# Attention values computed in strips of TensorE's columns, with the softmax scaling ahead of them

## What is computed

```python
# layer 0: layer norm with a conditioned scale and shift, 16 heads of 32, 4 key/value heads
scores = einsum('bhtd,bhsd->bhts', q, k_exp) / sqrt(32)
scores = where(mask, -inf, scores)      # window of 64, every 64th key, no later block of 128
y = einsum('bhts,bhsd->bhtd', softmax(scores), v_exp)
x = x + y @ Wo0.T
# layer 1: RMS norm with a conditioned scale, 8 heads of 64, 1 key/value head, no mask
ctx = einsum('bkgst,bktd->bkgsd', softmax(q k^T / 8), v)
x = x + ctx @ Wo1.T
x = x + silu(h @ Wg.T) * (h @ Wu.T) @ Wd.T      # 2048 inner features
```

## Time and profile before

| | us |
|---|---|
| median of three runs | 1804.08 |
| the profiled execution: its span | 1804.9 |
| TensorE busy | 1717.2 (95%) |
| VectorE busy | 1152.3 (64%) |
| ScalarE busy | 945.9 (52%) |
| GpSimd busy | 398.8 (22%) |
| a steady round (pairs 2 to 7) | about 210 |

### The profile page before, as it was taken

One profiled execution on the slowest core, in us unless ns is written; L12 is line 12 of the kernel. 1 busy time (PEld: TensorE's weight loads), 2 busy tenths in 40 slices (PEclk: granted clock), 3 DMA queues, 4 the chain that ended last, 5 costly groups with the idle time before them and its releaser, 6 DMA issues.

```text
span 1804.9 us, 37773 instructions
## 1 busy us (share of the span) xinstructions
PE 1717.2 (95%) x12440; PEld 931.9 (52%) x12440; DVE 1152.3 (64%) x2858; ACT 945.9 (52%) x2769; POOL 398.8 (22%) x556
## 2 busy tenths in 40 slices
PE   6686899999999999999999999999999999999999
PEld 2344445555455545555455554555455554555444
DVE  6759566675667657685576756676576855767320
ACT  3836456364664538564483646645385644835320
POOL 3438587011111112111110111111121111101120
PEclk9676999999999999999999999999999999999999
DMA  7866489462784449662593637944485725936220
GB/s 245 152 181 115 126 197 253 98 117 82 163 175 94 80 119 184 133 118 78 127 194 91 119 88 161 171 95 82 115 192 125 123 73 138 196 85 112 100 70 24
DMA packets 527231, 234.30 MB, mean 130 GB/s; under 512 B 476336, under 2 KB 493744, under 8 KB 527024
## 3 DMA queue, kind: packets, MB, share of 16 engines
q1 hardware_dynamic: 511472, 175.09, 48.9%
q10 hardware_dynamic: 15552, 56.63, 10.1%
HBM read 90.09 MB, written 16.78 MB: 59 GB/s over the span
## 4 chain that ended last, share of the span: by engine, by line
PE 77%; DVE 10%; DMA 6%; issue 4%; ACT 2%; SPq 1%; DVEq 0%; POOL 0%; ACTq 0%
PE up L1427 8%; PE up L1429 8%; PE up L1428 8%; PE gate L1427 7%; PE gate L1429 7%; PE gate L1428 7%; PE y L1427 4%; PE y L1428 4%; PE y L1429 4%; PE bank L1427 4%; PE bank L1429 4%; PE bank L1428 4%; DMA prob_t<-prob 3%; PE bank L1454 2%; DVE prob L1113 2%
## 5 line engine op out<-in xcount | busy, mean ns | idle before, releaser
L864 ACT ACTIVATE bank<-bank,low 128x128 f32<-128x128 f32 (+2 forms) x768 | 302.7, 395 | 68.2 <-DVE low L1106 35.0
L702 POOL TENSOR_TENSOR inner_t<-inner,inner_t 128x512 f16<-128x512 f32 x128 | 149.0, 1164 | 662.7 <-ACT inner_t L1045 662.6
L1113 DVE TENSOR_TENSOR prob<-bank,prob 128x512 f16<-128x512 f32 (+1 forms) x320 | 202.8, 634 | 54.3 <-ACT prob L873 53.4
L873 ACT ACTIVATE prob<-bank 128x512 f16<-128x512 f32 (+1 forms) x320 | 178.7, 558 | 73.3 <-DMA prob_t<-prob 44.5
L1427 PE MATMUL up<-mlp,ring 128*128 128x512 f16 x512 | 194.9, 381 | 12.8 <-DVE inner L1392 12.8
L1382 DVE SCALAR_TENSOR_TENSOR silu<-silu,gate 128x512 f32<-128x512 f32 x128 | 87.9, 687 | 183.8 <-ACT silu L1039 183.0
L1427 PE MATMUL gate<-mlp,ring 128*128 128x512 f16 x512 | 194.0, 379 | 1.4 <-DVE mlp L1078 0.9
L1429 PE MATMUL up<-mlp,ring 128*128 128x512 f16 x512 | 194.9, 381 | 0.0
L1428 PE MATMUL up<-mlp,ring 128*128 128x512 f16 x512 | 194.9, 381 | 0.0
L1429 PE MATMUL gate<-mlp,ring 128*128 128x512 f16 x512 | 194.0, 379 | 0.0
L1428 PE MATMUL gate<-mlp,ring 128*128 128x512 f16 x512 | 193.9, 379 | 0.0
(11 more groups left out here) (182 smaller groups left out, 4041.8 us busy)
## 6 DMA issues: line engine op xcount, KB each, us to landing
ring<-wgu_dram ACTq DMA_DIRECT2D x108, 512.0 KB, 3.8
x_in<-x_dram SPq DMA_DIRECT2D x18, 512.0 KB, 3.8
x_res<-x_mid SPq DMA_DIRECT2D x16, 512.0 KB, 3.0
wgu_dram<-ring SPq DMA_DIRECT2D x16, 512.0 KB, 3.6
out_dram<-x_res SPq DMA_DIRECT2D x32, 256.0 KB, 2.3
prob_t<-prob SPq DMA_TRANSPOSE x256, 3.5
inner_t<-wd_t_dram SPq DMA_DIRECT2D x4, 1024.0 KB, 8.7
ring<-wg_t_dram SPq DMA_DIRECT2D x16, 256.0 KB, 4.1
```

What stands on the lines that cost most here:

```text
L702: pool.tensor_tensor(inner_t[:, 1, f, :], inner[:], inner_t[:, 0, f, :], ALU.subtract).then_inc(inner_low, 1)
L864: ins = act.activation(bank_[:, at:at + wid], bank_[:, at:at + wid], ACT.Exp, bias=low[:, j % BANKS, k:k + 1], scale=-1.0, accum_out=total)
L873: act.activation(terms(prob[:, g % SLOTS, 0, :], layer, j), terms(work_bank[USE[f"unit{layer}", j] % BANKS][:], layer, j), ACT.Copy).then_ ...
L1113: dve.tensor_tensor(terms(prob[:, slot, 1, :], layer, j), terms(work_bank[USE[name] % BANKS][:], layer, j), terms(prob[:, slot, 0, :], lay ...
```

## The change

1. **Values in strips.** The values are now the stationary operand, 32 columns wide in layer 0 and 64 in layer 1, and the turned exponentials move past them, 512 or 256 columns at a time. The four key/value heads of layer 0 write to four different sets of 32 partitions of one bank, the two halves of layer 1's heads to two sets of 64. Four units make a batch (`batch_values`); units are ordered so that a batch belongs to one sequence and one set of 128 tokens.
2. **Scaling earlier.** The result now has the features in the partitions, as the projection wants it, so the division can no longer follow. `inverses` takes the reciprocals of a unit's sums on VectorE, and `prob_highs` and `prob_lows` scale by them, one instruction for each head.
3. **Gone:** `normalise` and the transposes `heads` on TensorE. ScalarE and VectorE split the result straight from its bank.
4. **Moved:** the output projection of the first 128 tokens, and its `add`, stand at the last two units of a layer, and not behind them.
5. **Beside it:** the turned exponentials have eight places and not five; the weight `wo0` has its rows in another order and is split on GpSimd; squares go to other buffers.

The core of the diff:

```diff
 UNIT = [
-    [(s, 0, [(4 * g + j, j * P, P) for j in range(4)]) for g in range(4) for s in BOTH]
-    + [(s, 1, [(2 * k + j, 2 * j * P, K_TWO) for j in range(2)]) for k in range(8) for s in BOTH],
+    [(s, 0, [(4 * g + j, j * P, P) for j in range(4)]) for s in BOTH for g in range(4)]
+    + [(s, 1, [(4 * g + 2 * pair + j, 2 * j * P, K_TWO) for j in range(2)])
+       for pair in range(2) for s in BOTH for g in range(4)],
     [(s, t, [(2 * k + j, j * TOK, TOK) for j in range(2)])
-     for t in range(TILES) for k in range(4) for s in BOTH]]
+     for t in range(TILES) for s in BOTH for k in range(4)]]
...
+BATCH = 4
+BATCHES = [units // BATCH for units in UNITS]
...
+TAKE_AT = [{BATCH * last_batch(layer, s, 0) + BATCH - 1 + LAG + 1: s for s in BOTH}
+           for layer in range(2)]
+OUT_AT = [{22: 0, 23: 1}, {14: 0, 15: 1}]
...
             def prob_highs(n, layer, j):
                 g = unit_index(layer, j)
-                need(act, terms_made, count(n, sum(UNITS), g + 1))
+                need(act, inv_ready, count(n, sum(UNITS), g + 1))
                 turned_before(act, n, g)
-                act.activation(terms(prob[:, g % SLOTS, 0, :], layer, j),
-                               terms(work_bank[USE[f"unit{layer}", j] % BANKS][:], layer, j),
-                               ACT.Copy).then_inc(hi_done, 1)
+                s, t, columns = UNIT[layer][j]
+                bank_ = work_bank[USE[f"unit{layer}", j] % BANKS]
+                for h, at, wid in columns:
+                    ins = act.activation(prob[:, g % SLOTS, 0, at:at + wid], bank_[:, at:at + wid],
+                                         ACT.Copy, scale=inv[:, s, t, h:h + 1])
+                ins.then_inc(hi_done, 1)
...
+                        if j in TAKE_AT[layer]:
+                            heads(n, layer, TAKE_AT[layer][j], 0)
...
             def prob_lows(n, layer, j):
                 name, slot = (f"unit{layer}", j), unit_index(layer, j) % SLOTS
                 need(dve, hi_done, count(n, HI_USES, HI_USE[name] + 1))
-                dve.tensor_tensor(terms(prob[:, slot, 1, :], layer, j),
-                                  terms(work_bank[USE[name] % BANKS][:], layer, j),
-                                  terms(prob[:, slot, 0, :], layer, j),
-                                  ALU.subtract).then_inc(prob_split, 1)
+                s, t, columns = UNIT[layer][j]
+                bank_ = work_bank[USE[name] % BANKS]
+                for h, at, wid in columns:
+                    ins = dve.scalar_tensor_tensor(
+                        prob[:, slot, 1, at:at + wid], bank_[:, at:at + wid],
+                        inv[:, s, t, h:h + 1], prob[:, slot, 0, at:at + wid], ALU.mult,
+                        ALU.subtract)
+                ins.then_inc(prob_split, 1)
+
+            def inverses(n, layer, j):
+                s, t, columns = UNIT[layer][j]
+                heads = slice(columns[0][0], columns[-1][0] + 1)
+                need(dve, terms_made, count(n, sum(UNITS), unit_index(layer, j) + 1))
+                dve.reciprocal(inv[:, s, t, heads],
+                               (sums0 if layer == 0 else sums1)[:, s, t, heads]).then_inc(
+                                   inv_ready, 1)
...
+                inverses(n, layer, 0)
...
+                    if j + 1 < total:
+                        inverses(n, layer, j + 1)
+                    if j in TAKE_AT[layer]:
+                        heads_low(n, layer, TAKE_AT[layer][j], 0)
+                    if j in OUT_AT[layer]:
+                        add(n, layer, OUT_AT[layer][j], 0)
...
             def finish(n, m, layer):
                 between(m, f"out{layer}a.0", f"out{layer}a.1")
-                for s in BOTH:
-                    add(n, layer, s, 0)
-                for s in BOTH:
-                    normalise(n, layer, s, 1)
                 between(m, f"heads{layer}.0", f"heads{layer}.1")
                 for s in BOTH:
...
+            HALVES = ((0, 0), (0, 1), (1, 0))
+
+            def batch_values(n, layer, b):
+                first = BATCH * b
+                s, t, _ = UNIT[layer][first]
+                for j in range(first, first + BATCH):
+                    g = unit_index(layer, j)
+                    need(pe, prob_in[g % TURNED], turned_count(n, g))
...
+                turned = turned_batch(batch_index(layer, b))
+                if layer == 0:
+                    heads = UNIT[0][first][2]
+                    out_cols = slice(heads[0][0] % 4 * P, (heads[-1][0] % 4 + 1) * P)
+                    blocks = ([(P, 0, slice(0, 4))] if t == 0 else
+                              [(P, 1, slice(0, 4, 2)), (K_NEAR, 2, slice(1, 4, 2))])
+                    for m, (rows, tile, places) in enumerate(blocks):
+                        for k, (of_v, of_p) in enumerate(HALVES):
+                            for g in range(KV0):
+                                ins = pe.matmul(
+                                    ybank[s][g * HD0:(g + 1) * HD0, out_cols],
+                                    v0[s][of_v][0:rows, tile, g * HD0:(g + 1) * HD0],
+                                    turned[0:rows, g, of_p, places, :], start=m == 0 and k == 0,
+                                    stop=m == len(blocks) - 1 and k == 2)
+                else:
+                    for m in range(TILES):
+                        for k, (of_v, of_p) in enumerate(HALVES):
+                            for j in range(2):
+                                ins = pe.matmul(
+                                    ybank[s][j * HD1:(j + 1) * HD1, :], v1[s][of_v][:, m, :],
+                                    turned[:, :, of_p, 2 * j + m, :], start=m == 0 and k == 0,
+                                    stop=m == TILES - 1 and k == 2)
                 ins.then_inc(pv_done, 1)
...
-                    if j in FILL_AT[layer]:
-                        heads(n, layer, FILL_AT[layer][j], 0)
-                    if j >= LAG:
-                        unit_values(n, layer, j - LAG)
+                    if j in OUT_AT[layer]:
+                        project(n, layer, OUT_AT[layer][j], 0, w)
+                    if (j - LAG) % BATCH == BATCH - 1 and j >= LAG:
+                        batch_values(n, layer, (j - LAG) // BATCH)
...
             def finish(n, m, layer, w):
-                last = range(UNITS[layer] - LAG, UNITS[layer])
-                for s in BOTH:
-                    unit_values(n, layer, last[s])
-                    between(m, f"out{layer}a.{s}")
-                    project(n, layer, s, 0, w)
-                for j in last[PAIR:]:
-                    unit_values(n, layer, j)
+                between(m, f"out{layer}a.0")
+                between(m, f"out{layer}a.1")
+                batch_values(n, layer, BATCHES[layer] - 1)
                 for s in BOTH:
                     between(m, f"heads{layer}.{s}")
-                    heads(n, layer, s, 1)
```

148 lines of the change are left out of this document (49 added, 99 removed).

## The result

The changed kernel takes 1952.05 us (median of four runs, 1949.3 to 1958.9), the kernel before 1803.69 beside it: 1.083 times as long, 95% interval 1.081 to 1.085. The forecast was 1971, slower. The profiled execution has a span of 1951.2 us against 1804.9.

The account below looks back on a forecast made before the run. Bound: the ScalarE-VectorE chain in the units, not TensorE. Six steady rounds (131 us) plus 18 for each of two others gave +167 on the 1804.9 span: 1972, as median 1971 us; range 1890 to 2035.

Parts of the forecast that it names:

- The chain: In the units, reciprocal, high halves, low halves and minima take turns between VectorE and ScalarE; 1971 us, chance 0.68 with concurrent strips.
- The steady round: Sum for one round with feed-forward: 14.3 + 9.7 + 1.3 - 3.4 = +21.9 us, six of them 131.
- Prices of the chain: Turns of 3.5 (four heads), 2.3 (two heads) and 2.5 us (layer 1); layer 0 +14.3, layer 1 +9.7 us.
- A turn with a gate: Layer 0: VectorE waits for a tanh begun behind the high halves, then needs 0.6 us itself; 1.08 each, eight gates 8.6.
- Edges: Layers' first units +0.8 and +0.5 us; TensorE's work behind the last units 2.1 less in layer 0, 1.3 in layer 1.
- The first two rounds: The round with the second pair and the one without feed-forward (no gates, cheaper minima): 18 us more each.
- Strips side by side: TensorE's value matmuls run four at a time in layer 0, two in layer 1; TensorE's sum 8.7 us less a round.
- a rival at 1734 us: TensorE stays the bound, ScalarE and VectorE keep their overlap across units, strips run concurrently: 1734 us, faster; chance 0.04.
- Moved projections: First tokens' projections run at the last two units in TensorE's waiting time; two projections, 5.2 us, remain behind the last unit.
- The profile's signs: TensorE's share some 85%, idle before scores; high halves wait for the reciprocal, low halves for high halves in nearly every unit.
- that sign: The prediction would be wrong if PEclk, TensorE's granted clock, stood under 1.00 in the units.
- the rival's 20 us a round: TensorE's clock falls in layer 1's units, 60 us against 39.6: 8 x 20 more, 2134 us; chance 0.06.

Follow-up runs that it names:

- the open kernel: Changed kernel, but ScalarE's high halves wait only for their unit's exponentials, not for VectorE's reciprocal, and are left unscaled by the row sum: 1817.0 us.

## Why the prediction was right

**The chain.** Shown. Taking the wait away gave back 135 of 148 us, and the chain stands in the timeline link by link as written. The steady round came out 20.8 us longer (mean of the five between the starts of the third and the eighth; 21.9 predicted), but 18.9 and 18.8 us in the two rounds without low clock outside the units. The prediction's sum had no term for that, so a part of the agreement is luck.

**Prices of the chain.** The turns were 3.37, 2.22 and 2.45 us against 3.48, 2.26 and 2.49. From the first to the last low halves in the round of the earlier trace rows layer 0 took 68.3 us (966.81 to 1035.08), +13.6 against 54.7, and layer 1 38.8 (1076.44 to 1115.20), +8.8 against 29.9. Predicted were +14.3 and +9.7. Pricing the instructions head by head from four scalings elsewhere held, within 0.11 us a turn. A turn with a gate took 4.46 instead of 3.37 and 3.31 instead of 2.22: 1.09 more, 1.08 predicted.

**Edges.** Between the last low halves of layer 0 and the first of layer 1 +0.1 us; between layer 1's last and the next round's first 82.3 (1115.20 to 1197.49) against 83.8, -1.5. By the prediction's terms -1.6 and -0.5. The first missed a piece of low clock, below: in the three rounds without one between the layers it came out at -1.4 to -1.8 (39.7, 39.7 and 39.4 us against 41.1 to 41.4 before).

**The first two rounds**, the mis-sized term: 18 each was taken, 11.0 and 13.2 measured. It was copied from the steady round less the gates. In the first round the units grew by 16.1 us, but the stretch between the layers shrank from 48.7 to 42.2. In the second, layer 0's units had already taken 67.8 us before, not 58.5, and grew by 7.7. Of the 20.8 us between the span forecast (1972) and the one measured, these two rounds make 11.8, five steady rounds 5 x 1.1 and the last round 3.2.

**Strips side by side.** Right: 0.78 us for the batch of which 0.65 was assumed. The size of their gain was not: I had 8.7 us less TensorE a round, 70 in all, and a rival at 1734 us for a kernel without the chain. With all that goes with them the strips give 33 us where nothing waits, 2.7 of them in a steady round, and the open kernel takes 1817. The rival failed for a second reason: without the chain the halves head by head alone cost 47 us. By the Trainium skill's page TensorEngine Tiling (Array Packing), section Theoretical Speedup, up to 4x was to be had with 32 columns; the trace agrees for the matmuls themselves (four starts within 0.01 us, then 0.11), and not for the kernel.

**Moved projections**: predicted to run in time that TensorE would have spent waiting, which took two projections (5.2 us) out of each layer's edge. Putting them back changed nothing that can be measured: with them back the step between the layers' low halves is 39.6 to 40.0 us in the rounds without low clock there, against 39.4 to 39.7. So the count of TensorE's work behind the last unit is not what sets the edges, and that their size came out as forecast is in part luck. **The profile's signs**: 88% for TensorE instead of some 85; high halves waiting for the reciprocal, as said; scores waiting for low halves, 52.0 us in layer 1. PEclk in the units was not 1.00 but 0.98 and 0.95: that sign said "wrong". The clock did fall, for short pieces, but the units took 68.3 and 34.3 us (first to last scores) in all six rounds from the third on, whether a piece fell in them or not; the rival's 20 us a round were not there.

## What to carry to other kernels

Before work is moved from the end of a stage into its middle, draw the loop that it closes: which engine must now wait for the other's last step of the same turn. Add the links of that loop and compare with the bound engine's time for a turn; busy shares (in layer 0 97% for TensorE, 82 and 77% for the others) say nothing about it. A wait and longer instructions were worth 33 and 47 us apart, and 165 together. Loosening one link won 90 us at best of the 135 that the whole wait cost, so look for what is second before moving anything.

## What the runs showed of the hardware

**Strips overlap even when the program has them one after the other.** Value matmuls to four strips, as neighbours, started 3 to 4 ns apart and cost one matmul's 0.11 us. In the order strip by strip a batch of 24 took 1.9 times as long with identical instructions, and a batch of 12 took 0.79 us against 0.77; in both, matmuls of a later strip started ahead of some that the program has before them. Whether the engine or a step before it changes the order, the trace does not say. The page TensorEngine Tiling (Array Packing) of the Trainium skill says in Key Properties that a change of tiling mode drains the engine; the trace agrees. Two scores of 193 columns, 0.08 us each, start from 1010.89, and the first value matmul at 1011.15 and not 1011.05; behind the last step the feed-forward starts another 0.10 late. So the two changes cost a batch about 0.2 us.

**The clock falls in short pieces.** The changed kernel's TensorE, before, in and behind one of them, in windows and in the timeline:

```profile
1080.00:1088.20 8.20, 4.95 (x33) 2.82 (x31) 6.37 (x19) 5.25 (x18) 0.88 (x2) 1.00 0.51 98
1088.20:1092.00 3.80, 3.80 (x12) 1.33 (x11) 2.99 (x10) 2.50 (x9) 1.71 (x5) 0.55 0.41 79
...
1089.08 0.63 PE L1439 MATMUL up<-wd_hi,inner_t 128*128 128x512 f16 x1
1089.51 0.63 PE L1440 MATMUL up<-wd_lo,inner_t 128*128 128x512 f16 x1
...
1092.17 0.38 PE L1441 MATMUL gate<-wd_hi,inner_t 128*128 128x512 f16 x1
1092.39 0.38 PE L1439 MATMUL gate<-wd_hi,inner_t 128*128 128x512 f16 x1
```

TensorE had been busy 4.95 of 8.2 us. Then matmuls of 512 columns started 0.43 us apart instead of 0.22, the lower level of 1.2 GHz for 2.4, for about 3.4 us while it was fully busy, and went back. That cost about 1.7 us of its work. There were three such pieces in this round. Inside the units they cost nothing that can be seen. In the open they do: the stretch between the layers in three rounds of the changed kernel, with two pieces, one (the fence in the section on the result) and none:

```profile
560.10:608.00 47.90, 44.62 (x277) 22.29 (x276) 28.39 (x77) 17.61 (x51) 4.09 (x6) 0.93 0.40 89
...
1257.10:1301.90 44.80, 41.55 (x277) 21.34 (x276) 28.36 (x76) 17.61 (x51) 4.09 (x6) 1.00 0.46 95
```

A piece of low clock costs 1.5 to 1.6 us there, and some 1.8 between layer 1 and the next round (83.2 and 83.3 us at 0.98, 81.5 and 81.3 at 1.00). From the third round on six pieces lie in the open; at these prices that is an estimate of 10 of the 148 us. They are not there in every kernel: from 330 to 1800 us the granted clock was 0.98 in the changed kernel and 1.00 in the kernel before, in the one with the wait alone and in the one without the wait. So taking the wait away took these pieces away too, and their 10 us are part of its 135. No run holds the clock still to measure them by themselves.

**What stays open**: why the open kernel takes 61 us in layer 0's units with TensorE busy for 56, ScalarE for 54 and VectorE for 50. From the first to the last low halves layer 0 took 58.8 us there and 61.4 in the kernel before with the halves head by head, against 54.7, so it goes with the halves head by head and not with the strips. ScalarE's waits for the turning transfers are seen, but make only 3.4 us in that stretch (more places for the halves were not tried), and no run separates them from the order of the feed-forward work.
